# A two-layer decoder on one core: 22 warming products from the last exponential on, twelve more between the convolution taps, and one unit that waits for one low half

## The chip, the cores and the metric

The kernel runs on one core of a Trainium2 chip. The metric is the device time of one execution, in microseconds (us). Before the change it is 2155.56 us, the median of three executions (2151.88 to 2157.25).

## What is computed

Four sequences (batches) of 512 tokens by 256 features go through two layers of a decoder: windowed attention, latent cross-attention with 8 heads of 128 over 1024 context tokens and 512 own ones, a ternary ("BitNet") feed-forward with a depthwise convolution of three taps, then self-attention and cross-attention with 16 heads of 16, and a routed feed-forward of eight experts. The parts around the change:

```python
x = x + _L0_xattn_ref(ctx_1024, _layernorm(x, axis=-1), ...)
x = x + _L0_ffn_ref(_layernorm(x, axis=-1), ...)
# _L0_ffn_ref:
h = bit_linear(x, w1)                    # quantised rows by ternary weights, 256 -> 1024
h = depthwise_conv1d(h.transpose(0, 2, 1), conv_w, conv_b)
h = jax.nn.silu(h.transpose(0, 2, 1))
return bit_linear(h, w2)                 # 1024 -> 256
```

## The kernel before, in words

One program, written out by hand for each engine; the four batches follow one another, and within a batch the stages `windowed`, `latent`, `bitnet`, `self_attention`, `cross_attention` and `routed`. Each engine has its own function for each stage, and semaphores tie them together; an engine does its instructions strictly in the order written. Nearly every float32 product is done as three float16 products of high and low halves (`product`, lines 650 to 657): one value "unit" is therefore computed by TensorE (PE), then its high half is written by ScalarE (`unit_hi`), then its low half by VectorE (`unit_lo`), which counts `u_lo`.

**The first head of `latent`.** For each head the seven units of the next head (keys 0 to 2, query 3, values 4 to 6) are computed between the score products of the current one. Each unit goes to PSUM bank 7, except unit 1 of the first head, which goes to bank 6. Before a unit is computed, `unit` waits for the count of `u_lo` that it is given as `free`, so that its bank is empty. In `head` (lines 819 to 836) step i does: scores of the next tile of 128 tokens, unit 2i, the weighted sum of tile i-1 (`weighted`: 24 products with the high halves of the transposed probabilities at lines 810 and 811, then 12 with their low halves at line 816), and unit 2i+1. `weighted` waits for two transposing DMAs, one for each half, issued by SyncE at lines 459 and 463 once ScalarE (line 1410) and VectorE (line 1821) have written that half. In the first head at i = 1, both unit 2 and the wait of line 830 ahead of `weighted` ask for the low half of unit 1, since `weighted` writes bank 6.

**The entry of `bitnet`.** The last head ends with products of line 795 to 797 (`project`); VectorE adds them to x (line 1900), counts `xo_added`, computes the moments and centres the rows, quantises them (lines 1939 to 1948), and PE turns the result with eight transposes (`transpose_y`, line 681). Between, PE runs 16 products that nobody reads (`keep_warm`, line 674, bank 4). Bank 4 is part of the score banks 3 to 5, which the last exponential of the stage reads.

**The taps.** The hidden layer has eight tiles of 128 channels. For each, PE makes four products of 512 columns (line 914) into one of four PSUM banks (`H_BANK` = 2, 3, 0, 1); ScalarE applies the middle tap (line 1471), VectorE the two outer ones (lines 1954 and 1959, the second counts `h_conv`), ScalarE the silu (line 1467, counts `h_silu`). From the fourth tile on PE follows each tile's products with two transposes of the tile three before (`early_transposes`, line 901, which waits for its silu), and after the eighth tile makes those of the last three (m = 5, 6, 7). They go to banks 4 to 7: tiles 0 to 3 to banks 4 and 6, tiles 4 to 7 to banks 5 and 7. Then come the quantisation of the hidden rows and the second product, which already have warming products of their own.

Of the kernel before, what the change touches and what calls it, by code (L numbers as in the profile page):

```python
# [23 lines left out]
NT = S // P  # L24
DC = D // P
HID = 1024
NM = HID // P
XH, XD = 8, 128
# [11 lines left out]
HB = 4  # L40
# [68 lines left out]
def decoder(nc, x_dram, ctx_dram, ctxT_dram, w_dram, moe_in, tern_in, col_in, row_in, b2_in, mask_in,  # L109
            rope_q_in, rope_k_in, ident_in, ident16_in, out):  # L110
    c_ = ExitStack()
    with c_:
# [3 lines left out]
        def sig(name, per_batch=0, credit=0):  # L116
            return Signal(nc, c_, name, per_batch, credit)
# [189 lines left out]
        s_mm, s_max, s_exp, s_rs = sig("s_mm", NTI), sig("s_max", NTI), sig("s_exp", NTI), sig("s_rs", NTI)  # L307
# [3 lines left out]
        xo_mm, xo_added = sig("xo_mm", 2), sig("xo_added", 2)  # L311

        h_mm, h_mid, h_conv, h_silu = sig("h_mm", NM), sig("h_mid", NM), sig("h_conv", NM), sig("h_silu", NM)
# [24 lines left out]
        def W(name, c, n0, n):  # L338

            width = next(w_ for k_, _, w_ in RESIDENT if k_ == name)  # L340
            at = OFF[name] + c * width + n0
            return wh[:, bass.ds(at, n)], wl[:, bass.ds(at, n)]
# [7 lines left out]
        def both(pair, *at):  # L350
            return tuple(t[at] for t in pair)
# [15 lines left out]
        H_BANK = (2, 3, 0, 1)  # L367
# [279 lines left out]
        def _(pe):  # L647
            mm = nc.tensor.matmul

            def product(out_, pairs):  # L650

                last, n = None, len(pairs)
                for k, ((lh, ll), (rh, rl_)) in enumerate(pairs):
                    mm(out_, lh, rh, start=(k == 0), stop=False)  # L654
                    mm(out_, lh, rl_, start=False, stop=False)  # L655
                    last = mm(out_, ll, rh, start=False, stop=(k == n - 1))  # L656
                return last
# [12 lines left out]
            def keep_warm(n, bank):  # L670


                for _ in range(n):
                    mm(ps[:, bank, :], ident16[:], wh[:, 0:512], start=True, stop=True)
# [86 lines left out]
            def unit(b, h, par, k, free, bank=7):  # L761


                if free is not None:
                    pe.wait_ge(u_lo.sem, u_lo.at(b, free))
                if k < 3:
                    last = product(ps[:, bank, :], [(W("xkv", c, h * XD, XD), both(cT, slice(None), c, slice(512 * k, 512 * k + 512)))
                                                 for c in range(DC)])
                elif k == 3:
                    last = product(ps[:, bank, :], [(W("xq", c, h * XD, XD), both(cT, slice(None), c, slice(NCTX, NKV)))  # L770
                                                 for c in range(DC)])
                else:
                    for t in range(4):
                        a0 = P * (4 * (k - 4) + t)
                        last = product(ps[:, bank, P * t:P * t + P],
                                       [(both(cT, slice(None), c, slice(a0, a0 + P)), W("xkv", c, h * XD + XIN, XD))
                                        for c in range(DC)])
                last.then_inc(u_mm.sem, 1)

            def scores(b, par, i, n=None):  # L780

                if n is not None:
                    pe.wait_ge(s_exp.sem, s_exp.at(b, n - 1))
                for t in range(3):
                    last = product(ps[:, 3 * (i % 2) + t, :], [(both(qT[par], slice(None), slice(P * i, P * i + P)),
                                                                both(kT[par], slice(None), slice(512 * t, 512 * t + 512)))])
                last.then_inc(s_mm.sem, 1)
# [31 lines left out]
            def head(b, h, par, first_head=False):  # L819
                for i in range(NT):  # L820
                    n = h * NT + i
                    if i < NT - 1:
                        scores(b, par, i + 1, None if first_head and i == 0 else n + 1)
                    else:
                        pe.wait_ge(u_lo.sem, u_lo.at(b, 7 * (h + 1) + 4))
                        scores(b, 1 - par, 0, n + 1)
                    unit(b, h + 1, 1 - par, 2 * i, 7 * (h + 1) + 2 * i)
                    if i:
                        if first_head and i == 1:
                            pe.wait_ge(u_lo.sem, u_lo.at(b, 7 * (h + 1) + 2))  # L830
                        weighted(b, i - 1, h, par)
                    elif not first_head:
                        weighted(b, NT - 1, h - 1, 1 - par)
                    if i < NT - 1:
                        second = first_head and i == 0
                        unit(b, h + 1, 1 - par, 2 * i + 1, 7 * (h + 1) + (0 if second else 2 * i + 1), 6 if second else 7)
# [53 lines left out]
                last_head(b, XH - 1, 1)  # L890

            def bitnet(b):
                pe.wait_ge(xo_added.sem, xo_added.at(b, 2))
                keep_warm(16, 4)
                transpose_y(b, 1)

                def early_transposes(m):

                    pe.wait_ge(h_silu.sem, h_silu.at(b, m + 1))
                    for i in range(2):  # L900
                        last = nc.tensor.transpose(ps[:, G_BANK[i] + m // 4, P * (m % 4):P * (m % 4) + P],
                                                   g[:, m, P * i:P * i + P], ident[:])
                        if m == NM - 1:
                            last.then_inc(g_t.sem, 1)

                for m in range(NM):
                    if m >= HB:
                        pe.wait_ge(h_conv.sem, h_conv.at(b, m - HB + 1))
                    for part in range(2):
                        for c in range(DC):  # L910
                            if m == 0:
                                half = (y_hi, y_lo)[part]
                                pe.wait_ge(half.sem, half.at(b, 2 * 1 + c + 1))
                            last = mm(ps[:, H_BANK[m % HB], :], tern[:, 0, HID * c + P * m:HID * c + P * m + P],
                                      yT[part][:, c, :], start=(c + part == 0), stop=(c + part == 2))
                    last.then_inc(h_mm.sem, 1)
                    if m >= 3:
                        early_transposes(m - 3)
                for m in range(NM - 3, NM):
                    early_transposes(m)  # L920
                pe.wait_ge(h_conv.sem, h_conv.at(b, NM))
                for i in range(2, NT):
                    if i == NT - 1:
                        keep_warm(7, G_BANK[i])
                    for m in range(NM):
                        last = nc.tensor.transpose(ps[:, G_BANK[i] + m // 4, P * (m % 4):P * (m % 4) + P],
                                                   g[:, m, P * i:P * i + P], ident[:])
                    last.then_inc(g_t.sem, 1)
                for j in range(NT + 1):
                    if j == 1:  # L930
                        keep_warm(6, GQ_BANK[j])
                    if j < NT:
                        pe.wait_ge(g_quant.sem, g_quant.at(b, j + 1))
                        if j == 0:
                            pe.wait_ge(g_scaled.sem, g_scaled.at(b, 1))
                        if j >= 2:
                            pe.wait_ge(gq_done.sem, gq_done.at(b, j - 1))
                        dst = ps[:, GQ_BANK[j % 2], :].bitcast(F16)
                        for m in range(NM):
                            last = nc.tensor.transpose(dst[:, P * m:P * m + P], gi[:, j % 2, P * m:P * m + P], ident16[:])  # L940
                        last.then_inc(gq_t.sem, 1)
                    if j >= 1:
                        i = j - 1
                        pe.wait_ge(gq_done.sem, gq_done.at(b, i + 1))
                        if i == 0:
                            pe.wait_ge(g_scaled.sem, g_scaled.at(b, 2))
                        if i >= 2:
                            pe.wait_ge(f_added.sem, f_added.at(b, i - 1))
                        for m in range(NM):
                            last = mm(ps[:, F_BANK[i % 2], 0:D], gq[:, m, P * i:P * i + P], tern[:, 1, D * m:D * m + D],  # L950
                                      start=(m == 0), stop=(m == NM - 1))
                        last.then_inc(f_mm.sem, 1)
# [1363 lines left out]
```

## Time and profile before

| | |
|---|---|
| median of three executions | 2155.56 us |
| lowest, highest | 2151.88, 2157.25 us |
| the profiled execution's own time | 2158.11 us |
| its span | 2156.3 us |
| PE busy | 1954.7 us, 91% |
| VectorE (DVE) busy | 1721.8 us, 80% |
| ScalarE (ACT) busy | 1310.9 us, 61% |
| GpSimd (POOL) busy | 263.7 us, 12% |
| mean granted TensorE clock | 0.992 of full |

The profile is of one execution. Times of rows count from the start of the span. A row of the timeline gives start, duration, engine, line, operation, tiles and number of instructions; in square brackets behind it stands how long the engine sat idle before it, and what ended that. The ends of PE's products are modelled, so consecutive starts say more of its pace than durations do. The granted clock is 1.00 at 2.4 GHz and 0.50 at 1.2 GHz; a value between them in a short window means that the clock changed inside it.

### The profile page before, as it was taken

The page shows a single profiled execution, that of the slowest core. Times are in us where ns is not written, and L with a number is a line of the kernel's source. Part 1 is how long each engine was busy: PE and PEld are TensorE (multiplying, and loading weights), DVE is VectorE, ACT ScalarE, POOL GpSimd, SP SyncE. Part 2 cuts the span into 40 slices and gives each one's busy share as a digit, 9 for nine tenths or more (in the row PEclk, how much of TensorE's full clock was granted, in tenths as well). Part 3 has the DMA queues.
Part 4 walks back from the last instruction along what each step waited for, and adds up shares of the span by engine and source line. Part 5 has one row for each costly group of instructions (what it writes and reads, how often), then busy time and mean ns, then how long its engine had stood idle before and what let it go on. Part 6 is the DMA issues. An engine that isn't in the chain of part 4 may idle for free.

```text
span 2156.3 us, 42882 instructions
## 1 busy us (share of the span) xinstructions
PE 1954.7 (91%) x17870; PEld 1106.2 (51%) x17870; DVE 1721.8 (80%) x2681; ACT 1310.9 (61%) x1953; POOL 263.7 (12%) x280
## 2 busy tenths in 40 slices
PE   1999988989999997888999999798999999889898
PEld 0577753323657774232466766333256777533235
DVE  7888878696888887779588887869868888786956
ACT  3566656578356665738636764574944666555682
POOL 2000001242000000135100000103500000011430
PEclk9999999999999999999999999999999999999999
DMA  6166630021036671002005666002101666400200
GB/s 272 38 126 126 133 79 12 9 94 31 20 74 126 126 140 36 11 13 108 11 21 111 129 128 130 10 5 78 45 11 42 126 126 127 99 12 9 94 2 11
DMA packets 424210, 156.39 MB, mean 73 GB/s; under 512 B 405928, under 2 KB 416560, under 8 KB 423120
## 3 DMA queue, kind: packets, MB, share of 16 engines
q1 hardware_dynamic: 423440, 151.54, 29.8%
q8 instruction: 141, 2.31, 0.5%
q0 software_dynamic: 576, 2.10, 0.3%
q14 instruction: 53, 0.43, 0.1%
HBM read 43.43 MB, written 2.16 MB: 21 GB/s over the span
## 4 chain that ended last, share of the span: by engine, by line
PE 61%; DVE 28%; ACT 5%; issue 3%; DMA 2%; POOL 0%; POOLq 0%; SPq 0%; DVEq 0%; ACTq 0%
DVE nmx L2009 14%; PE ps L654 11%; PE ps L656 11%; PE ps L655 11%; PE ps L1019 6%; PE ps L816 4%; PE ps L810 3%; PE ps L811 3%; PE ps L1005 3%; DMA arena<-arena 2%; PE ps L972 1%; DVE st L1653 1%; DVE arena L1821 1%; PE ps L1029 1%; PE ps L1086 1%
## 5 line engine op out<-in xcount | busy, mean ns | idle before, releaser
L2009 DVE TENSOR_REDUCE nmx<-ps 128x2 f32<-128x1024 f32 x384 | 445.0, 1219 | 16.2 <-PE ps L972 14.7
L1516 ACT ACTIVATE arena<-ps 128x512 f32<-128x512 f32 x768 | 406.1, 600 | 52.1 <-PE ps L1005 47.3
L654 PE MATMUL ps<-arena 128*128 128x512 f16 (+1 forms) x784 | 267.1, 341 | 1.3 <-DVE arena L1745 1.1
L655 PE MATMUL ps<-arena 128*128 128x512 f16 (+1 forms) x784 | 266.7, 340 | 0.0
L656 PE MATMUL ps<-arena 128*128 128x512 f16 (+1 forms) x784 | 266.7, 340 | 0.0
L1808 DVE TENSOR_SCALAR_CACHE_REDUCE ps<-ps 128x1536 f32<-128x1536 f32 x128 | 225.7, 1764 | 41.9 <-PE ps L656 41.3
L1019 PE MATMUL ps<-arena 128*17 128x256 f32 x3072 | 241.5, 391 | 0.0
L1821 DVE SCALAR_TENSOR_TENSOR arena<-arena,rs 128x1536 f16<-128x1536 f32 x128 | 231.6, 1810 | 4.2 <-ACT arena L1410 4.2
L1410 ACT ACTIVATE arena<-arena,rs 128x1536 f16<-128x1536 f32 x128 | 200.8, 1569 | 42.9 <-DVE rs L1814 42.9
L1403 ACT ACTIVATE arena<-ps,nm 128x1536 f32<-128x1536 f32 x128 | 197.1, 1540 | 10.5 <-DVE ps L1808 10.5
L626 POOL TENSOR_TENSOR rstd<-ve,col 128x2 f32<-128x2 f32 x40 | 29.3, 732 | 1289.7 <-DVE ve L1914 868.5
L810 PE MATMUL ps<-arena 128*128 128x128 f16 x1536 | 185.3, 219 | 1.3 <-DMA arena<-arena 1.2
L811 PE MATMUL ps<-arena 128*128 128x128 f16 x1536 | 185.3, 219 | 0.0
L972 PE MATMUL ps<-arena 64*128 64x512 f16 x768 | 151.2, 387 | 25.3 <-DVE nmx L2009 16.7
L1005 PE MATMUL ps<-arena 64*128 64x512 f16 x768 | 169.8, 392 | 2.8 <-ACT arena L1516 1.7
L654 PE MATMUL ps<-wh,arena 128*128 128x128 f16 (+2 forms) x864 | 153.9, 221 | 3.3 <-ACT arena L1529 1.8
L810 PEld LDWEIGHTS ps<-arena 128*128 128x128 f16 x1536 | 150.3, 98 | 8.9 <-issue 1.3
L811 PEld LDWEIGHTS ps<-arena 128*128 128x128 f16 x1536 | 150.3, 98 | 7.2
L656 PE MATMUL ps<-wh,arena 128*128 128x128 f16 (+2 forms) x864 | 153.6, 221 | 0.0
L655 PE MATMUL ps<-wl,arena 128*128 128x128 f16 (+2 forms) x864 | 153.6, 221 | 0.0
L1005 PEld LDWEIGHTS ps<-arena 64*128 64x128 f16 x768 | 48.9, 93 | 165.1 <-ACT arena L1516 133.8
L654 PE MATMUL ps<-arena,wh 128*128 128x512 f16 x312 | 118.4, 380 | 8.9 <-DVE arena L1743 7.1
(285 smaller groups left out, 3725.0 us busy)
## 6 DMA issues: line engine op xcount, KB each, us to landing
arena<-in_experts SPq DMA_DIRECT2D x4, 3840.0 KB, 11.5
arena<-in_weights SPq DMA_DIRECT2D x8, 929.0 KB, 12.4
arena<-arena SPq DMA_DIRECT2D x72, 64.0 KB, 2.1
arena<-in_ctx SPq DMA_DIRECT2D x4, 1024.0 KB, 6.1
arena<-arena SPq DMA_TRANSPOSE x256, 3.2
arena<-in_ctx_t SPq DMA_DIRECT2D x4, 1024.0 KB, 4.8
arena<-arena SPq DMA_DIRECT2D x72, 32.0 KB, 1.9
arena<-in_ternary SPq DMA_DIRECT2D x2, 1024.0 KB, 6.1
```

Source lines behind the costliest of these rows:

```text
L654: mm(out_, lh, rh, start=(k == 0), stop=False)
L655: mm(out_, lh, rl_, start=False, stop=False)
L656: last = mm(out_, ll, rh, start=False, stop=(k == n - 1))
L810: mm(d_, vh[:, kt, :], ph[:, kt, :], start=(kt == 0), stop=False)
L811: mm(d_, vl[:, kt, :], ph[:, kt, :], start=False, stop=False)
L1005: mm(ps[:, 4 + n % 3, :], ks[rows, 2 * g_ + pp, P * kt:P * kt + P], qs[rows, 2 * g_ + pp, :], start=True, stop=True).then_inc(b_mm.sem, 1)
L1019: mm(ps[32 * j:32 * j + VW, 7, cols], v17[:, kt, 4 * g_ + j, :], pr_[:, (4 * t + j) % RING, cols], start=(kt + half == 0), stop=(kt == mod ...
L1410: A(xq[i % 2][0], xp[:, i % 2, :], ACT.Copy, scale=rs[:, i:i + 1]).then_inc(s_hi.sem, 1)
L1516: A(pr_[:, n % RING, :], ps[:, 4 + n % 3, :], ACT.Exp).then_inc(b_exp.sem, 1)
L1808: TS_(s_, s_, -XS, None, ALU.mult, ALU.min, accum_out=nm[:, i:i + 1]).then_inc(s_max.sem, 1)
L1821: STT(xq[i % 2][1], xp[:, i % 2, :], rs[:, i:i + 1], xq[i % 2][0], ALU.mult, ALU.subtract).then_inc(s_lo.sem, 1)
L2009: V.tensor_reduce(nmx[:, g_ % 2, ch, :, pp, i], ps[:, 2 * (z % 2):2 * (z % 2) + 2, :], AX.X, ALU.max, negate=True)\
```

## The change

Four edits, all in PE's program. In the first head the third unit (unit 2, at i = 1) waits for the low half of unit 0 and no longer for that of unit 1. At the entry of `bitnet` PE waits for the last exponential in place of the second addition to x, and makes 22 warming products, not 16. Four warming products into bank 5 come after the products of the fourth hidden tile. After the eighth tile PE waits until five tiles have had their taps, and makes four warming products into bank 2 ahead of the transposes of tile 5 and four ahead of those of tile 6. The other engines' programs stay as they are.

```diff
-                    unit(b, h + 1, 1 - par, 2 * i, 7 * (h + 1) + 2 * i)
+                    unit(b, h + 1, 1 - par, 2 * i, 7 * (h + 1) + (1 if first_head and i == 1 else 2 * i))
...
             def bitnet(b):
-                pe.wait_ge(xo_added.sem, xo_added.at(b, 2))
-                keep_warm(16, 4)
+                pe.wait_ge(s_exp.sem, s_exp.at(b, NT * XH))
+                keep_warm(22, 4)
                 transpose_y(b, 1)
...
                     last.then_inc(h_mm.sem, 1)
+                    if m == 3:
+                        keep_warm(4, 5)
                     if m >= 3:
                         early_transposes(m - 3)
+                pe.wait_ge(h_conv.sem, h_conv.at(b, HB + 1))
                 for m in range(NM - 3, NM):
+                    if m < NM - 1:
+                        keep_warm(4, H_BANK[0])
                     early_transposes(m)
```

## Rows read from the trace of the kernel before

**Rows 1.** The page: busy time of each engine.
```profile
PE 1954.7 (91%) x17870; PEld 1106.2 (51%) x17870; DVE 1721.8 (80%) x2681; ACT 1310.9 (61%) x1953; POOL 263.7 (12%) x280
```

**Rows 2.** Timeline of PE in batch 0, first head: start, duration, line, [idle before].
```profile
96.92 0.39 PE L654 MATMUL ps<-arena,wh 128*128 128x512 f16 x1 [1.77 <-DVE arena L1743]
...
98.22 0.22 PE L810 MATMUL ps<-arena 128*128 128x128 f16 x1
...
99.56 0.83 PE L816 MATMUL ps<-arena 128*128 128x128 f16 x12
```

**Rows 3.** Timeline of PE, first head of batches 1 and 2.
```profile
618.96 0.39 PE L654 MATMUL ps<-arena,wh 128*128 128x512 f16 x1 [1.77 <-DVE arena L1743]
...
623.10 0.84 PE L816 MATMUL ps<-arena 128*128 128x128 f16 x12 [1.33 <-DMA arena<-arena]
...
1142.70 0.39 PE L654 MATMUL ps<-arena,wh 128*128 128x512 f16 x1 [1.77 <-DVE arena L1743]
```

**Rows 4.** Window in batch 0's latent stage: length, PE, PEld, DVE, ACT, POOL busy, PEclk.
```profile
161.70:215.60 53.90, 53.90 (x597) 38.62 (x595) 45.79 (x64) 37.21 (x44) 0.00 (x0) 1.00 0.65 126
```

**Rows 5.** Timeline of PE, from the last head of batch 0 through its taps.
```profile
292.34 0.27 PE L797 MATMUL ps<-wh,arena 128*128 128x256 f16 x1
293.89 3.63 PE L674 MATMUL ps<-wh,ident 128*128 128x512 f16 x16 [1.28 <-DVE x L1900]
298.19 1.75 PE L681 MATMUL ps<-ident,y 128*128 128x128 f32 x8 [0.68 <-DVE y L1948]
300.52 0.88 PE L914 MATMUL ps<-yT_hi,tern 128*128 128x512 f16 x2 [0.58 <-ACT yT_hi L1352]
...
306.07 0.44 PE L901 MATMUL ps<-ident,arena 128*128 128x128 f32 x2 [1.25 <-ACT arena L1467]
...
311.66 0.44 PE L901 MATMUL ps<-ident,arena 128*128 128x128 f32 x2
313.12 0.44 PE L901 MATMUL ps<-ident,arena 128*128 128x128 f32 x2 [1.02 <-ACT arena L1467]
314.62 0.44 PE L901 MATMUL ps<-ident,arena 128*128 128x128 f32 x2 [1.06 <-ACT arena L1467]
```

**Rows 6.** Windows of 1 us where the clock changed: PE, PEld, DVE, ACT, POOL busy, PEclk.
```profile
315.00:316.00 1.00, 0.78 (x5) 0.72 (x5) 0.33 (x1) 0.23 (x1) 0.00 (x0) 0.73 0.00 0
...
318.00:319.00 1.00, 1.00 (x4) 0.34 (x3) 0.93 (x5) 0.57 (x2) 0.00 (x0) 0.56 0.00 0
...
1349.00:1350.00 1.00, 0.57 (x2) 0.20 (x2) 0.69 (x2) 0.76 (x2) 0.00 (x0) 0.85 0.00 0
...
1871.00:1872.00 1.00, 0.65 (x3) 0.21 (x3) 0.77 (x2) 0.69 (x2) 0.00 (x0) 0.97 0.00 0
```

**Rows 7.** Windows from `bitnet`'s first transpose to self-attention's, batches 0 to 3; PEclk is granted clock.
```profile
298.19:330.67 32.48, 25.43 (x154) 14.50 (x154) 26.74 (x59) 21.97 (x28) 0.99 (x2) 0.95 0.03 13
822.17:854.05 31.88, 23.92 (x153) 13.28 (x153) 26.83 (x59) 22.20 (x28) 0.98 (x2) 1.00 0.03 12
1347.00:1379.96 32.96, 25.35 (x153) 13.60 (x154) 26.82 (x59) 22.19 (x28) 0.99 (x2) 0.95 0.03 12
1868.92:1901.88 32.96, 25.49 (x154) 13.65 (x154) 26.84 (x59) 22.19 (x28) 0.99 (x2) 0.95 0.03 12
```

**Rows 8.** Timeline of DVE, first head of batch 0: low halves of unit 0 and of unit 1.
```profile
93.46 0.75 DVE L1743 SCALAR_TENSOR_TENSOR arena<-ps,col,arena 128x512 f16<-128x512 f32 x1 [0.49 <-ACT arena L1358]
...
96.12 0.74 DVE L1743 SCALAR_TENSOR_TENSOR arena<-ps,col,arena 128x512 f16<-128x512 f32 x1
```

**Rows 9.** Timeline of SP: the first low-half transposing DMA of batches 0, 1, 2.
```profile
95.97 1.29 SPq L463 DMA_TRANSPOSE arena<-arena  x1
...
618.01 1.39 SPq L463 DMA_TRANSPOSE arena<-arena  x1
...
1141.75 1.40 SPq L463 DMA_TRANSPOSE arena<-arena  x1
```

**Rows 10.** Line 463 over the whole run: its DMAs from issue to landing.
```profile
DMA to landing us min/median/max: 3.2/3.2/5.0
```

## The prediction, made before the changed kernel was run

> **What bounds the kernel now.** I read the page first. PE is busy 91% of the span and DVE 80% [rows 1], so an edit of PE's program counts where PE is the engine that the others wait for, and hardly elsewhere. The timeline of PE then says which kind each edited place is. In the first head PE stands still for 1.77 us until DVE has written a low half [rows 2]; the same wait, to the hundredth, is in the other batches [rows 3]. Behind it PE has no idle time for long: in a window in the middle of the stage it is busy for all of 53.90 us, DVE for 45.79 [rows 4]. A shift of PE there moves the rest of the batch. At the entry of `bitnet` it is the other way: PE waits 1.28 us for the addition, then 0.68 us for the quantised rows, then 0.58 us for the high half [rows 5]. The chain runs over DVE and ACT there, and PE's idle time costs nothing by itself. So it is in the taps, where PE waits 1.25, 1.02 and 1.06 us for silus [rows 5].
>
> What PE's idleness can cost is its clock. The mean over the span is 0.992 and hides where it fell, so I asked for the granted clock in windows of 1 us. It fell to half in three of the four `bitnet` stages: in batch 0 late, behind the taps, at about 315.5 and back at about 318.9 (0.73 of a window and 0.56 of one), and in batches 2 and 3 at the entry, at about 1349.7 and 1871.9 [rows 6]. The stage windows price this. Batch 1 kept a clock of 1.00 and took 31.88 us from its first transpose to the next stage's; batch 0 took 32.48, batches 2 and 3 took 32.96 each [rows 7]. A late fall costs 32.48 - 31.88 = 0.60 us, an entry fall 32.96 - 31.88 = 1.08 us, and all three together 0.60 + 2 x 1.08 = 2.76 us. That is all that warming can win inside these stages.
>
> **Part 1, the unit.** Unit 2 asked for unit 1's low half, which ends at 96.12 + 0.74 = 96.86. It now asks for unit 0's, ready at 93.46 + 0.75 = 94.21 [rows 8]. PE is free at 96.92 - 1.77 = 95.15, so the unit starts there without a wait. Six products of 0.216 us (98.22 - 96.92 = 1.30 us for the six) [rows 2] end it at 96.45. The next step, `weighted`, still waits for unit 1's low half (line 830), so it can't start before 96.92; it started at 98.22. A first wait of 0.47 us stays. Its 24 high-half products take 99.56 - 98.22 = 1.34 us, so they end at 98.26. Next are the 12 low-half products, which need the transposing DMA. That was issued at 95.97 [rows 9], after a DVE instruction which the change doesn't move, and the shortest and the median landing of that line is 3.2 us [rows 10]: 99.2. Before, PE came to it at 99.56, when it had just landed, and no wait showed. Now PE is there at 98.26 and waits 0.9 us. So of 1.77 us only 99.56 - 99.2 = 0.36 us is gained. In batch 2 issue and unit are 1142.70 - 1141.75 = 0.95 us apart, as in batch 0 (96.92 - 95.97) [rows 2, 3, 9], and I take batch 3 alike. In batch 1 the DMA landed only at 623.10, some 5.1 us after its issue at 618.01, and PE already waited 1.33 us for it [rows 3, 9]; an earlier unit gives nothing. Sum: 3 x 0.36 = 1.1 us.
>
> Does this gain last? Unit 3, behind the weighted sum, now wants to start at 99.9. It needs unit 2's low half; its high half can follow when ACT ends the scaled tile, and DVE takes it behind the next maximum, by about 99.4 as I lay the rows out, so it isn't late. From there the order and the distances are the old ones. I take the 0.36 us through to the end of the stage. The bounds of this part are 0 (a late landing in every batch) and 1.30 us per batch, 5.2 in all (the landing were no bound).
>
> **Part 2, the entry.** The new wait costs nothing: the last exponential feeds weighted sums that PE itself has ended before its last product of line 797 at 292.34 [rows 5]. Nothing is queued behind it that could be delayed. PE starts warming at about 292.45, not at 293.89. 16 products took 3.63 us, so 22 take at most 22/16 x 3.63 = 4.99 us and end by 297.44; the first transpose starts at 298.19, set by DVE. Cost nothing, with 0.7 us to spare. The warming's end hardly moves: it was 293.89 + 3.63 = 297.52. What the six extra products fill is the gap of 1.28 us in front. The two entry falls came later, behind the gaps of 0.68 and 0.58 us and between short transposes that come at DVE's pace, and those stay as they are. So I expect the entry falls to be as frequent as before: 0 us. Bounds: a gain of 2 x 1.08 = 2.2 us if both vanish, a loss of as much if the other two batches get one as well.
>
> **Part 3, between the taps.** Four warming products take 4/16 x 3.63 = 0.91 us. The gaps that they go into are 1.25, 1.02 and 1.06 us [rows 5]; each fits, by 0.1 us at the least. The added wait for the fifth tile's taps is over before the transposes of tile 4 at 311.66, since those wait for the same tile's silu, which follows its taps. Behind that wait stand the warming products and the transposes of tile 5, which aren't ready before 313.12. Cost: nothing at full clock. The cover is the wait for the silu; if DVE's taps were faster by 0.1 us, warming would begin to show. The late fall of batch 0 came right behind the gaps of 1.02 and 1.06 us, with two short transposes between them. These gaps are filled, so I expect no late fall any more. In the profiled execution that is 0.60 us. The fall came in one batch of four though the same gaps are in all, so where it strikes is chance; an execution can have none or four, 0 to 2.4 us. For a usual one I take two, 1.2 us.
>
> The Trainium skill (TensorE: Matmul & The Clock Gate, the table of the two states) says that the clock drops after an idle stretch. By that rule short gaps don't matter and all warming here is worth nothing: the sum would be part 1 alone. The same page's section on depth-cycling says that small idle times between groups of products do make it swing; the three falls behind gaps of 0.6 to 1.3 us agree with this one and not with the table.
>
> **The sum.** Against the profiled execution's own time: 2158.11 - 1.1 - 0.6 = 2156.4 us. That execution lies 2158.11 - 2155.56 = 2.55 us above the median of the three. Against the median, with two late falls in a usual execution: 2155.56 - 1.1 - 1.2 = 2153.3 us. A difference of 0.3% is 6.5 us, about the least that a measurement of this kernel can tell from no change; the three runs themselves spread over 5.4 us.
>
> **The rivals.** First, nothing at all. The falls have nothing to do with the short gaps that are filled and come as often as before, and the early unit is swallowed by the landing, as in batch 1. Then 2155.6. (The first half of this is the Trainium skill's table, TensorE: Matmul & The Clock Gate.) For it speaks that only one late fall is on record. Against it, that the landing leaves 0.36 us in the other batches. With part 1 kept, it is 2155.56 - 1.1 = 2154.5. Second, more than I count: the landing is no bound in the first head, 4 x 1.30 = 5.2 us, and all falls go, 2.76 us: 2155.56 - 8.0 = 2147.6. Against it speaks the 3.2 us, the least of that line's landings [rows 10]. Third, slower: the clock falls shortly before the entry, and the warming products, which can't be called off, run at half of it. A fall lasts about 3.4 us [rows 6], which holds 8 products of 0.43 us in place of 16; the 22 then end some 8 x 0.216 = 1.7 us later, at 299.1, against rows that are ready at 298.19: 0.95 us late, and between the taps four products take 1.73 us against gaps of 1.02 to 1.25, 0.5 to 0.7 us late, three times. All of it in every batch is 4 x (0.95 + 1.9) = 11 us: 2167. It decides from a low clock at 292 on; the record has no fall near there, and PE comes to 292.34 out of a row of products, which is why I give it little.
>
> **How the numbers follow.** My forecast, a gain of 1 to 4 us: 0.72. Nothing at all, 2154.5 to 2155.6: 0.18. More than I count: 0.07. Slower: 0.03. The first two both lie within 0.3%, so faster by over 0.3% has 0.07, within 0.3% has 0.90, slower 0.03. The range runs from 2149.5 (the forecast with both entry falls gone, and half of part 1's upper end) to 2156.5 (no gain, and one fall more).
>
> **What would show it.** In the profile of the changed kernel: unit 2 starts at about 95.15 with no wait, the first product of line 810 at about 96.9, and a new idle time of about 0.9 us ahead of line 816, put down to the DMA; from 100 us on everything is 0.36 us earlier. If that idle time is missing, part 1 is worth more. At the entry the 22 products run from 292.45, the transposes come as before behind DVE, and the gap ahead of them is 0.8 to 0.9 us. Between the taps the gaps shrink to about 0.1 to 0.4 us, the stage window without a fall stays at 31.88 us, and no clock of 0.5 follows the taps. Entry falls, 1.08 us each, are still to be seen in about half of the batches. A stage window above 31.9 us at a clock of 1.00 would mean that the warming costs something after all, and late falls in several batches would prove the gaps innocent.

## The result, and the profile after

The changed kernel takes 2159.53 us, the median of twelve executions (2154.67 to 2163.75), against 2153.55 us for the kernel before in twelve beside them (2149.70 to 2158.48). The ratio is 1.0025, with a 95% interval of 1.0016 to 1.0034: slower by about 5.4 us. Forecast were 2153.3 us and a range that ended at 2156.5; the measured time lies above it. Ratios here and below are estimated from all executions of both kernels and need not equal the ratio of the medians; two executions that ran in a slow state, one of e8 (2837.71 us) and one of the kernel before beside it (3251.7 us), are left out of them.

The two profiled executions hide this. That of the changed kernel has a span of 2155.9 us (its own time is 2157.69, below its median), that of before had 2156.3 (2158.11, above its median). So I read both by stage, not as a whole. First the way from the latent stage's first transpose to `bitnet`'s, in windows of the changed kernel's trace, batches 0 to 3 (length, busy time of PE, PEld, DVE, ACT and POOL, granted clock, DMA share, GB/s):

```profile
78.66:301.62 222.96, 215.15 (x2279) 152.62 (x2279) 182.10 (x266) 139.01 (x161) 1.46 (x2) 0.99 0.59 119
603.20:824.69 221.49, 215.46 (x2279) 152.60 (x2279) 182.19 (x266) 139.12 (x161) 1.45 (x2) 0.99 0.58 120
1127.25:1345.97 218.72, 213.95 (x2279) 151.78 (x2279) 182.11 (x266) 139.01 (x161) 1.46 (x2) 1.00 0.58 122
1647.45:1870.78 223.33, 215.70 (x2279) 152.30 (x2279) 182.09 (x266) 139.00 (x161) 1.45 (x2) 0.99 0.58 119
```

The same windows of the kernel before:

```profile
78.80:298.19 219.39, 212.54 (x2272) 151.22 (x2272) 182.25 (x266) 139.08 (x161) 1.46 (x2) 1.00 0.60 121
600.85:822.17 221.32, 212.90 (x2273) 151.06 (x2273) 182.26 (x266) 139.09 (x161) 1.45 (x2) 1.00 0.58 120
1124.59:1347.00 222.41, 214.15 (x2272) 151.93 (x2273) 182.34 (x266) 139.20 (x161) 1.46 (x2) 0.99 0.59 119
1649.60:1868.92 219.32, 212.56 (x2272) 151.07 (x2272) 182.25 (x266) 139.09 (x161) 1.45 (x2) 1.00 0.58 121
```

Batches 0 and 3 became 3.6 and 4.0 us longer. Batch 2 became 3.7 us shorter, mostly because a wait late in that stage of before isn't there, in which the clock fell too (from 1315.6 us):

```profile
1316.00 1.46 PE L816 MATMUL ps<-arena 128*128 128x128 f16 x12 [2.75 <-DMA arena<-arena]
```

Batch 1 hardly moved: the late first landing of before is gone there, and a wait of 2.56 us for such a DMA came up at 793.7 us, again with a fall of the clock. DVE's and ACT's busy times are what they were. PE's rose by 2.6 us in batch 0 and by 3.1 in batch 3, because its clock fell in them, as shown below; the rest is waits that moved.

Here is the first head of batch 0 after the change, in PE's timeline; it answers to [rows 2]:

```profile
96.77 0.23 PE L810 MATMUL ps<-arena 128*128 128x128 f16 x1 [0.48 <-DVE arena L1748]
...
101.12 1.46 PE L816 MATMUL ps<-arena 128*128 128x128 f16 x12 [2.84 <-DMA arena<-arena]
```

The stall of 1.77 us ahead of the unit is gone. The short one of 0.48 ahead of line 810 is the one foretold as 0.47. But the wait for the low-half DMA is 2.84 us, not 0.9. That DMA was issued in its old place, and SyncE's timeline shows nothing odd (it answers to [rows 9]):

```profile
95.82 1.29 SPq L463 DMA_TRANSPOSE arena<-arena  x1
```

It landed some 5.2 us later, at 101.1, and during the wait the clock fell. Windows of 1 us, as in [rows 6]:

```profile
100.00:101.00 1.00, 0.00 (x0) 0.00 (x0) 0.96 (x3) 0.11 (x2) 0.00 (x0) 0.72 0.27 52
103.00:104.00 1.00, 1.00 (x5) 0.32 (x3) 0.00 (x0) 0.00 (x0) 0.00 (x0) 0.57 0.58 127
1670.00:1671.00 1.00, 1.00 (x10) 0.54 (x8) 0.00 (x0) 0.00 (x0) 0.00 (x0) 0.79 0.32 70
```

It was half from 100.4 to 103.9 in batch 0. In batch 3 the first landing was late too (4.85 us), and the clock fell 1.1 us behind the wait, at 1670.6. In this stage PE sets the pace, and a fall costs more than the 0.6 or 1.1 us in `bitnet`: some 1.4 us, by the comparison with e9 below.

Why did the DMA land late? The DMA view of its flight names the queues that were active. First before, from 95.9 to 99.3 us, then after, from 95.8 to 101.1:

```profile
q1 hardware_dynamic: 1820, 0.46, 59.3%
```

```profile
q1 hardware_dynamic: 2391, 0.60, 85.0%
q8 instruction: 1, 0.02, 1.9%
q14 instruction: 1, 0.01, 0.4%
```

Two fetches of instructions lie in the flight after the change, and none before. In the records of before they start at 100.4 and 100.5 us, 1.2 us after the landing; now at 98.0 and 98.5. The q8 fetch I take for PE's own: there are 141 in the run, and PE has 17,870 products and as many weight loads, which is one fetch for some 253 of them. Whose the q14 fetch is was not found out. PE's program reached the same place sooner, since it no longer stood in front of the unit.

The warming edits did what was said. PE in batch 0, from the entry through the taps, after the change; it answers to [rows 5]:

```profile
295.87 4.91 PE L674 MATMUL ps<-wh,ident 128*128 128x512 f16 x22
301.62 1.75 PE L681 MATMUL ps<-ident,y 128*128 128x128 f32 x8 [0.84 <-DVE y L1953]
...
308.09 1.03 PE L674 MATMUL ps<-wh,ident 128*128 128x512 f16 x4
309.50 0.44 PE L901 MATMUL ps<-ident,arena 128*128 128x128 f32 x2 [0.38 <-ACT arena L1472]
...
315.37 1.03 PE L674 MATMUL ps<-wh,ident 128*128 128x512 f16 x4
316.55 0.44 PE L901 MATMUL ps<-ident,arena 128*128 128x128 f32 x2 [0.16 <-ACT arena L1472]
316.82 1.03 PE L674 MATMUL ps<-wh,ident 128*128 128x512 f16 x4
318.05 0.44 PE L901 MATMUL ps<-ident,arena 128*128 128x128 f32 x2 [0.20 <-ACT arena L1472]
```

All warming fits into the waits: what is left of the gaps of 1.28, 1.25, 1.02 and 1.06 us is 0, 0.38, 0.16 and 0.20. And the stage windows of `bitnet` after the change, which answer to [rows 7]:

```profile
301.62:333.50 31.88, 26.52 (x165) 14.39 (x165) 26.82 (x59) 22.18 (x28) 0.98 (x2) 1.00 0.03 13
824.69:857.66 32.97, 27.99 (x165) 14.72 (x166) 26.84 (x59) 22.18 (x28) 0.99 (x2) 0.95 0.03 11
1345.97:1377.86 31.89, 26.52 (x166) 14.37 (x166) 26.83 (x59) 22.19 (x28) 0.99 (x2) 1.00 0.03 10
1870.78:1902.67 31.89, 26.53 (x166) 14.39 (x166) 26.82 (x59) 22.18 (x28) 0.99 (x2) 1.00 0.03 12
```

31.88 us at full clock, as batch 1 of before; one entry fall, no late one. In these two profiles the latent stage lost 4.1 us in the four batches (886.50 against 882.44), `bitnet` gained 1.7 (128.63 against 130.28) and all the rest of the program gained 2.8. So the one place of loss that they show is the latent stage; how the 5.4 us of the medians spread over the stages, a single profile of each can't say.

### The profile page after: what moved, and what is told of

Read it like the earlier page. It is cut to its first block, busy times and chain, and to the rows that moved or that the text cites. A ratio compares the mean times of both kernels' runs of the same rounds, so it can differ in the third digit from the quotient of the medians.

```text
span 2155.9 us, 43026 instructions
## 1 busy us (share of the span) xinstructions
PE 1970.2 (91%) x17942; PEld 1113.4 (52%) x17942; DVE 1720.0 (80%) x2681; ACT 1310.6 (61%) x1953; POOL 263.4 (12%) x280
## 4 chain that ended last, share of the span: by engine, by line
PE 62%; DVE 28%; ACT 5%; issue 3%; DMA 2%; POOL 0%; POOLq 0%; SPq 0%; DVEq 0%; ACTq 0%
DVE nmx L2014 14%; PE ps L654 11%; PE ps L656 11%; PE ps L655 11%; PE ps L1024 6%; PE ps L816 4%; PE ps L810 3%; PE ps L811 3%; PE ps L1010 3%; DMA arena<-arena 2%; PE ps L977 1%; DVE st L1658 1%; PE ps L1091 1%; PE ps L1034 1%; DVE quant L1928 1%
## 5 line engine op out<-in xcount | busy, mean ns | idle before, releaser
L810 PE MATMUL ps<-arena 128*128 128x128 f16 x1536 | 185.3, 219 | 4.1 <-DMA arena<-arena 2.2
L811 PE MATMUL ps<-arena 128*128 128x128 f16 x1536 | 185.3, 219 | 0.0
L816 PE MATMUL ps<-arena 128*128 128x128 f16 x1536 | 108.0, 221 | 15.3 <-DMA arena<-arena 15.3
```

The costliest lines, as they stand in the source:

```text
L810: mm(d_, vh[:, kt, :], ph[:, kt, :], start=(kt == 0), stop=False)
L811: mm(d_, vl[:, kt, :], ph[:, kt, :], start=False, stop=False)
```

## The experiments

Theory A: the earlier unit is the loss. It lets PE's instruction fetch fall into the flight of a transposing DMA that PE is about to need, with no slack left, and the longer wait can bring the clock down. Which batches are hit depends on the number of PE instructions ahead of them, and the warming edits change that number. Rivals were that the warming costs something itself (B, E), that the unit's new order costs whatever the fetches do (C), and that gains of the warming edits are gains of the clock (D). Each kernel was timed in turns with the kernel before, 8 to 12 executions of its own. The medians of the kernel before were 2155.33 us beside e1 to e4, 2155.98 beside e5 to e8 and 2154.83 beside e9 to e12, so medians compare directly only within such a group.

| kernel | median, us | ratio to before | 95% interval |
|---|---|---|---|
| e1 unit alone | 2158.84 | 1.0008 | 0.9998 to 1.0018 |
| e2 entry and taps | 2156.49 | 1.0002 | 0.9993 to 1.0011 |
| e3 taps alone | 2153.50 | 0.9988 | 0.9980 to 0.9997 |
| e4 entry alone | 2152.29 | 0.9982 | 0.9973 to 0.9990 |
| e5 changed kernel, padded by 64 | 2156.69 | 1.0002 | 0.9993 to 1.0011 |
| e6 before, padded by 64 | 2152.58 | 0.9982 | 0.9973 to 0.9991 |
| e7 before, six narrow products | 2151.06 | 0.9982 | 0.9973 to 0.9991 |
| e8 changed kernel, gap filled | 2158.04 | 1.0009 | 1.0000 to 1.0018 |
| e9 unit, 18 narrow products | 2158.78 | 1.0016 | 1.0007 to 1.0024 |
| e10 before, 18 narrow products | 2155.59 | 1.0004 | 0.9995 to 1.0013 |
| e11 unit, padded by 84 | 2149.26 | 0.9978 | 0.9967 to 0.9988 |
| e12 before, padded by 84 | 2150.34 | 0.9980 | 0.9971 to 0.9989 |

### One part at a time: e1 to e4

**e1**, the kernel before with the unit's edit only:

```diff
-                    unit(b, h + 1, 1 - par, 2 * i, 7 * (h + 1) + 2 * i)
+                    unit(b, h + 1, 1 - par, 2 * i, 7 * (h + 1) + (1 if first_head and i == 1 else 2 * i))
```

> The kernel before with the edit of the unit alone. Theory A (the unit edit is the loss): in the first head of batch 0 the earlier unit lets PE's instruction fetch come at 98.0 us and not at 100.4, into the flight of the first low-half transposing DMA (issued 95.8); it lands some 5.2 us after its issue and not 3.2, PE waits over 2 us ahead of line 816, and often the clock falls behind that wait. The way from the latent stage's first transpose to bitnet's is then 221 to 223 us in batch 0 against 219.4 before, about 219 in batches 2 and 3; in all 2 to 5 us slower than before. Theory B (the warming edits of bitnet are the loss, the unit gains as predicted): 1 us faster, 219.0 in batch 0.

Its latent windows, batches 0 to 3:

```profile
78.53:300.15 221.62, 212.71 (x2273) 151.18 (x2273) 182.11 (x266) 139.02 (x161) 1.45 (x2) 1.00 0.59 120
601.56:825.05 223.49, 214.59 (x2272) 151.51 (x2272) 182.09 (x266) 139.02 (x161) 1.46 (x2) 0.99 0.58 119
1127.51:1349.73 222.22, 214.55 (x2273) 152.04 (x2273) 182.22 (x266) 139.14 (x161) 1.46 (x2) 0.99 0.58 120
1652.54:1871.55 219.01, 212.81 (x2273) 151.05 (x2273) 182.11 (x266) 139.02 (x161) 1.45 (x2) 1.00 0.59 121
```

This is the cleanest comparison, since the number of instructions is that of before. Batch 0 is 2.23 us longer (late landing, no fall), batch 1 2.17 us (late as before the change, a longer wait and a fall), and batch 3, where the landing was on time, 0.31 us shorter. There PE's timeline has the waits as they were foretold:

```profile
1670.65 0.23 PE L810 MATMUL ps<-arena 128*128 128x128 f16 x1 [0.47 <-DVE arena L1743]
...
1672.95 0.84 PE L816 MATMUL ps<-arena 128*128 128x128 f16 x12 [0.79 <-DMA arena<-arena]
```

Batch 2 has a late wait with a fall in both kernels (here at 1318.4), and so stays near 222. Both theory A and the gain of the prediction are in one trace: -0.3 us where the DMA is on time, +2.2 us where it is not. The total is less sharp: 3.5 us by the medians, 0.08% by the ratio, whose interval reaches 1.

**e2** has the entry and the taps as in the changed kernel, **e3** the taps alone, **e4** the entry alone; their edits are the parts of the diff above.

> The kernel before with the three warming edits of bitnet, the unit as before. Theory A: within 1.5 us of before, on the faster side; the bitnet stage windows take 31.9 us where the clock stays up, and no fall follows the taps. Theory B: about 5 us slower, either because a stage window is above 31.9 us at full clock, or because 36 more PE instructions per batch and their waits move PE's instruction fetches of batches 1 to 3 onto transposing DMAs that PE waits for.

> The kernel before with the twelve products between the taps alone. Theory A: 0 to 2 us faster (late clock falls of 0.6 us each gone in 0 to 4 batches). Theory B: slower by 2 us or more, as 24 more PE instructions per batch move the fetches.

> The kernel before with the entry's edit alone (wait for the last exponential, 22 products). Both theories: no change of the stage itself, entry falls (1.08 us each) as frequent as before. Theory A: within 1 us of before. Theory B: 1 us or more slower through moved fetches.

e2 is no different from before. That and e1 fit theory A and not B. But e3 gained 0.12% and e4 0.18%, which for e4 is outside the 1 us that I had allowed, and together (e2) they gained nothing. Costs of separate places would add up. What doesn't add up is where the instructions come to lie: e3 adds twelve products per batch (24 instructions of PE, with their weight loads), e4 six, e2 eighteen, so batches 1 to 3 get their fetches in other places. In e4 two of the stage windows have late falls and two have entry falls (32.49, 32.96, 32.49 and 32.95 us), so its gain isn't in `bitnet` at all; its latent windows sum to 878.85 us against 882.44 of before.

### The place of the instructions against warming: e7, e9, e10

**e7** adds to the kernel before six products of 8 columns at the entry, as many instructions as e4 adds:

```diff
                 keep_warm(16, 4)
+                for _ in range(6):
+                    mm(ps[:, 4, 0:8], ident16[:], wh[:, 0:8], start=True, stop=True)
```

> The kernel before with six products of 8 columns behind the 16 warming ones at bitnet's entry, under the old wait: as many PE instructions as the entry edit adds, and no warming to speak of. The entry edit alone ran at 0.9982 of before. Theory A (its gain is the place of the fetches in batches 1 to 3, not the clock): again 2 to 4 us faster than before, with the same fetch places as in the entry edit's trace. Rival D (its gain is the clock kept up by warming): no faster than before.

Its ratio is e4's: 0.9982, and in both traces the one late first landing is batch 1's, with PE's fetch 2.7 us behind the issue. So the gain of e4 is had with its instruction count alone; the warming had no part in it that can be seen (D falls).

**e9** is the changed kernel with narrow products at all the places of the added warming, and with the entry's old wait; **e10** is the same without the unit's edit.

```diff
+            def narrow(n, bank):
+                for _ in range(n):
+                    mm(ps[:, bank, 0:8], ident16[:], wh[:, 0:8], start=True, stop=True)
...
                 keep_warm(16, 4)
+                narrow(6, 4)
...
+                    if m == 3:
+                        narrow(4, 5)
...
+                pe.wait_ge(h_conv.sem, h_conv.at(b, HB + 1))
                 for m in range(NM - 3, NM):
+                    if m < NM - 1:
+                        narrow(4, H_BANK[0])
```

> The unit's edit, and at the places of the 6 and the 12 added warming products as many of 8 columns: the changed kernel's PE instruction count and order to the instruction, with next to none of its warming. Theory A (the loss is the unit's edit together with where the fetches fall; warming is worth little): as slow as the changed kernel, 4 to 6 us above before, with the first low-half DMA late (4.8 us or more) in batches 0 and 3. Rival E (the loss is the warming products' own cost): at most 2 us above before.

> The same 18 narrow products per batch without the unit's edit: the instruction places of the run with bitnet's edits alone, which came out at 1.0002 of before. Theory A: within 2 us of that run and so of before, no late first low-half landing, apart from late clock falls behind the taps, 0.6 us each, which can be back. If it is faster than before by 2 us or more, the warming itself costs something.

e9 came out at 1.0016 and e10 at 1.0004. Between them stands the unit's edit alone, and it costs 3.2 us by the medians. The two intervals overlap a little, but the two were timed in the same group, and their means lie 3.4 us apart with a standard error of about 1. That is 3.4 to 4.0 us above before, where I had expected 4 to 6. Most of the changed kernel's loss is there with next to no warming: E falls as the main cause. In e10 against e2 (1.0004 and 1.0002) no cost of the warming products can be seen. Windows of the latent stage, first e9, then e10:

```profile
78.53:300.04 221.51, 212.85 (x2278) 151.47 (x2279) 182.06 (x266) 139.00 (x161) 1.46 (x2) 1.00 0.59 120
...
1646.74:1868.65 221.91, 213.02 (x2278) 151.48 (x2278) 182.05 (x266) 139.00 (x161) 1.46 (x2) 1.00 0.59 120
```

```profile
79.09:298.51 219.42, 212.67 (x2279) 151.46 (x2279) 182.19 (x266) 138.99 (x161) 1.46 (x2) 1.00 0.58 121
...
1644.01:1864.34 220.33, 212.84 (x2278) 151.47 (x2278) 182.18 (x266) 139.00 (x161) 1.45 (x2) 1.00 0.60 121
```

As expected, batches 0 and 3 are the ones with the late first landing (5.26 and 4.70 us). In batch 3 of e9 the low-half DMA is issued at 1663.90, and PE gets to its products at

```profile
1668.65 0.84 PE L820 MATMUL ps<-arena 128*128 128x128 f16 x12 [2.28 <-DMA arena<-arena]
```

4.7 us later (line 820 there is line 816 here). In the flight (DMA view, 1663.9 to 1668.6) lies one fetch of PE:

```profile
q1 hardware_dynamic: 2399, 0.61, 79.7%
q8 instruction: 1, 0.02, 1.3%
```

In e10 that fetch comes 3.02 us after the issue, not 2.70, and the landing is on time. The two kernels have the same instructions in the same order. That the 0.3 us decide is not shown: in batch 1 of the kernel before the fetch came 3.05 us after the issue, and the landing took 5.04.

### Other places: e5, e6, e11, e12

Padding at the program's start, in e5 and e6 of 16 products (64 instructions of PE, for a float32 product is two loads and two products), in e11 and e12 of 21:

```diff
             mm(ps[:, 0, 0:2], ones, wsum[:], start=True, stop=True).then_inc(t_all.sem, 1)
+            for _ in range(16):
+                mm(ps[:, 4, 0:2], ones, wsum[:], start=True, stop=True)
```

> The changed kernel with 16 tiny float32 products that nobody reads (64 PE instructions) at its very start, where PE is idle for 30 us. They cost nothing themselves; they let every instruction fetch of PE, one per 256 of its instructions, come 32 products earlier in the program. Theory A (fetches that fall on the first low-half transposing DMA make the loss): the fetch that came 19.8 us behind the stage's first transpose in batch 0 and 20.0 in batch 3 comes 7 us earlier or more and misses the DMA; it lands 3.2 us after issue in all four batches; the way from the latent stage's first transpose to bitnet's is at most 219.0 in batches 0 and 3 unless another landing is late; median 3 to 6 us below the changed kernel's. Rival C (the earlier unit costs by its order, whatever the fetches): as slow as the changed kernel.

> The kernel before with the same 64 tiny PE instructions at its start. By themselves they cost nothing. Theory A: whatever time it differs from before by is due to fetches on other transposing DMAs; in the first head no landing is late; between 3 us faster and 2 us slower than before. Rival C: no difference at all from before, since no order changes.

e5 is a miss in its detail. I expected the padding to carry the fetches of batches 0 and 3 out of the flight, and it didn't: they came at 18.4 us behind the first transpose in both, still inside it (the flight is from 17.2 to 20.4), and the landings took 6.0 and 5.3 us. PE runs ahead in its program only up to the next wait, so a fetch moves less in time than in instructions. Batches 0 and 3 were as bad as ever and batches 1 and 2 good:

```profile
78.98:303.62 224.64, 216.76 (x2278) 152.87 (x2278) 182.07 (x266) 138.99 (x161) 1.46 (x2) 0.98 0.59 118
606.11:825.53 219.42, 214.03 (x2278) 151.79 (x2279) 182.08 (x266) 139.01 (x161) 1.45 (x2) 1.00 0.59 121
1128.03:1345.99 217.96, 213.90 (x2278) 151.73 (x2278) 182.06 (x266) 139.02 (x161) 1.46 (x2) 1.00 0.58 122
1648.85:1871.36 222.51, 215.39 (x2278) 152.69 (x2279) 182.07 (x266) 138.99 (x161) 1.46 (x2) 0.99 0.60 120
```

That the median fell all the same, from 1.0025 to 1.0002, must then lie in other places of the program; I can't say in which. e6 shows the size of such effects: 64 instructions that do nothing, in time in which PE is idle, make the kernel before 0.18% faster, 3.4 us by the medians. In its trace the late landing has wandered with the fetch to batch 0 (4.75 us), against what I had expected, while batch 1's has no fetch and is on time.

> The unit's edit alone, with 84 tiny PE instructions at the program's start that cost nothing and move PE's fetches to other places in all batches. If the first low-half landing is on time (3.2 us) in a batch, the way from the latent stage's first transpose to bitnet's is 0.3 us shorter than that batch has in the run with the same padding and without the edit; if it is late, that batch is 1.3 to 3.6 us longer. Theory A: the median follows the number of late ones: with none, 1 us below the padded kernel before; with two, 3 us above.

> The kernel before with the same 84 tiny PE instructions at its start, for comparison with the padded unit edit. Between 4 us faster and 2 us slower than before, by where the fetches fall; a late first low-half landing costs this order 1.0 to 1.5 us in a batch, since PE comes to it 1.3 us later.

With 84 instructions the places are good for both: 0.9978 and 0.9980, for e12 a little more than the 4 us that I had expected at most. Latent windows of e11, then of e12:

```profile
79.00:298.64 219.64, 212.74 (x2272) 151.15 (x2272) 182.06 (x266) 138.99 (x161) 1.46 (x2) 1.00 0.60 121
601.57:819.81 218.24, 212.80 (x2273) 151.16 (x2273) 182.06 (x266) 138.99 (x161) 1.46 (x2) 1.00 0.58 122
1121.10:1341.69 220.59, 212.90 (x2272) 151.09 (x2273) 182.05 (x266) 139.01 (x161) 1.46 (x2) 1.00 0.59 121
1643.10:1861.59 218.49, 212.91 (x2272) 151.12 (x2273) 182.05 (x266) 139.00 (x161) 1.46 (x2) 1.00 0.60 122
```

```profile
78.37:297.60 219.23, 212.55 (x2272) 151.16 (x2272) 182.21 (x266) 139.00 (x161) 1.46 (x2) 1.00 0.59 121
600.46:819.97 219.51, 212.59 (x2272) 151.11 (x2272) 182.18 (x266) 139.01 (x161) 1.45 (x2) 1.00 0.58 121
1122.58:1343.79 221.21, 212.73 (x2273) 151.07 (x2273) 182.19 (x266) 139.00 (x161) 1.45 (x2) 1.00 0.59 120
1646.83:1864.95 218.12, 212.49 (x2272) 151.04 (x2273) 182.18 (x266) 139.00 (x161) 1.45 (x2) 1.00 0.60 122
```

The unit's edit is 1.1 us ahead in the sum of the four windows (876.96 against 878.07) and by the medians, less than the timing can tell from nothing. So C falls: with the fetches elsewhere no cost of the earlier unit can be seen. The batches don't each follow the 0.3 us that I expected. In batch 0 the small fetch (q14) again moved up, from 21.5 to 19.3 us behind the first transpose, and the landing took 3.9 us; that batch is 0.4 us longer. Batch 3 is also 0.4 us longer without a late first landing; there it is a wait further on. e11 is faster than the kernel before, as e3, e4, e6, e7 and e12 are, but its twin e12 is so too: it gains by its instruction places, not by the change.

### The clock: e8

Five warming products of 384 columns in the new idle time. They start new sums in bank 6 beside an open one, so that tile 0's weighted sum of the first head isn't the reference's; order and times are otherwise the changed kernel's.

```diff
+            def fill():
+                for _ in range(5):
+                    mm(ps[:, 6, P:4 * P], ident16[:], wh[:, 0:3 * P], start=True, stop=True, skip_group_check=True)
...
-                        weighted(b, i - 1, h, par)
+                        weighted(b, i - 1, h, par, fill if first_head and i == 1 else None)
```

> The changed kernel with five warming products of 384 columns (0.16 us each at full clock) in the first head, between the high-half and the low-half products of tile 0, in the new idle time ahead of line 816. Theory A says that of the 3.6 us lost in batch 0, 2.2 are the late landing, which stays, and 1.3 to 1.4 the clock fall behind the idle time, which should go: no clock fall within 5 us of a first head's line 816, batch 0 at about 221.4 to 221.7, median 1 to 3 us below the changed kernel's. If the falls come all the same, the idle time is not what brings them.

The first heads had no fall, though the landings of batches 0 and 3 were as late as in the changed kernel (5.25 and 4.70 us); batch 0:

```profile
98.78 0.98 PE L821 MATMUL ps<-wh,ident 128*128 128x384 f16 x5
101.77 0.84 PE L816 MATMUL ps<-arena 128*128 128x128 f16 x12 [2.02 <-DMA arena<-arena]
```

The ratio fell from 1.0025 to 1.0009. By the ratios that is 3.4 us, a little over the expected 1 to 3, but the two intervals overlap, and e8's ten more instructions per batch have moved places as well. Batch 0 took 222.42 us, not 221.4 to 221.7, since another DMA wait of 1.28 us came up at 92 us into it. Over all profiles with the earlier unit and no filling, the clock fell behind five of the nine late first landings (changed kernel 2 of 2, e1 1 of 2, e5 2 of 2, e9 0 of 2, e11 0 of 1) and behind none of the eleven on time. With a fall behind about half of the late ones, two without a fall come by chance in one case of five. So e8 fits the view that filling keeps the clock up here, and doesn't show it.

## Why the prediction was wrong

**The unit (part 1).** The waits were right to 0.1 us where the DMA was on time: 0.47 and 0.79 us against 0.47 and 0.9, a gain of 0.31 us against 0.36. The step that failed is the sentence that takes the landing at 3.2 us in batches 0, 2 and 3 and reads the one late landing, batch 1's, as a fact of that batch. The row of line 463 gave a longest landing of 5.0 us [rows 10], and I asked neither what makes a landing late nor whether the edit moves it. Late landings were no rarity in the kernel before: of its 256, 44 took more than 3.6 us. That batches 0, 2 and 3 had theirs on time was the luck of its instruction places. And the edit moves them: "a DVE instruction which the change doesn't move" was said of the issue, while PE's own fetch, which shares the DMA engines, comes earlier when PE does. In batch 0 that turned 0.36 us of gain into 2.2 us of loss.

**What was cover.** PE used to reach line 816 1.3 us later and so had 0.36 us of slack even against a landing on time. A late landing of 4.7 to 5.0 us cost a wait of 1.0 to 1.3 us in the order before (before, e3, e4, e6 and e7, one batch in each), and in the new order one of 4.7 to 6.0 us cost 2.3 to 3.6 us (the 3.9 us of e11: 1.5). In the old order none of these five brought the clock down, in the new one five of nine did. The old order spends its idle time in two pieces, 1.77 us and at most 1.33, with products between, the new one most of it in one; a single wait of 2.75 us brought the clock down in the kernel before as well, at 1316. Behind a late landing, the stall that the change removed was paid at another place in full.

**The entry (part 2): right.** The 22 products end before the rows are ready, the falls came as often as before: 7 in 20 stage windows with 22 products, 9 in 36 with 16, over all profiles.

**The taps (part 3): right in kind, small in size.** No late fall (32.4 to 32.5 us) in the 20 windows with the warming between the taps, 12 in the 36 without. At 0.6 us each that is 0.8 us per execution; I had taken 1.2. Filling these three gaps of 1.0 to 1.25 us ended these falls. So the rule of the Trainium skill (TensorE: Matmul & The Clock Gate, table of the two states), that the clock drops after an idle stretch, is too narrow for this trace; its section on depth-cycling agrees with it.

**The rivals.** The slower one had 0.03 and the wrong mechanism, warming at half clock that delays the stage. It isn't in the trace: no stage window of `bitnet` was above 32.97 us. "More than I count" had more weight than a loss by the very DMA that I had named as the bound.

**The sum.** 2159.53 - 2153.55 is 6.0 us by the medians and 5.4 by the ratio. The forecast was a gain of 2.3 us on 2155.56, the median of three; twelve executions put that median at 2153.55, which is not where the forecast went wrong. Of the loss the unit's edit at these instruction places is 0.12%, 2.6 us (1.0016 against 1.0004; 3.2 by medians). The step from e9 to the changed kernel, 1.0016 to 1.0025, is open: the intervals overlap, and a fall behind a late landing, worth 1.4 us a batch (222.96 against e9's 221.51 in batch 0, 223.33 against 221.91 in batch 3), could fill it by chance. The rest is what the number of instructions does to places further on, which e10 (1.0004) bounds to little.

## What to carry to other kernels

Before a wait is moved up on an engine with a long straight program, ask of the next DMA that it will wait for not the usual landing but the late one, and what cover it loses. A small edit's gain or loss of 0.2% means little until a twin with as many instructions that do nothing has been timed: here three of four twins of the unchanged kernel (e6, e7, e12) ran about 4 us faster with no work of use changed, and the fourth (e10) did not move. Warming products that ended before what was waited for had no cost that these timings show.

## What the runs showed of the hardware

A transposing DMA in whose flight a fetch of instructions falls is often late, and hardly ever otherwise. Over the profiles of all fourteen kernels (3584 landings of the two transposing lines), 645 took more than 3.6 us, and 601 of these had a fetch start within 3.2 us of their issue; of the 2398 without a fetch 44 were late. A fetch doesn't always go with a delay: 585 that had one were on time, as batch 3 of e10. Of the 56 first low-half landings, 16 of the 17 with a fetch were late and none of the 39 without; where padding or the unit's edit moved the fetch (e6, e9, e11, e12), the late landing moved with it. In the late first landings that I looked at, the traffic goes on as a thin tail of some 10 GB/s after it had run at up to 290, as though one of the sixteen engines still worked off its share; that it is the fetch's engine was not tested.
